# Token lists from SBUF marks, the weights' sort between tiles, and first-batch gathers and additions in the experts' last blocks

## What is computed

```python
x = x + _L0_xattn_ref(_layernorm(x), ctx_2048, ...)
x = x + _L0_ffn_ref(_layernorm(x), gate_weight, w_gate, w_up, w_down)
x = x + _L1_xattn_ref(_layernorm(x), ctx_2048, mask)
x = x + _L1_ffn_ref(_layernorm(x), gate_w, up_w, down_w, gate_s, up_s, down_s)

# the experts (E = 64, K = 8 of them per token, I = 192)
scores = softmax(x @ gate_weight.T)
topk_w, topk_idx = top_k(scores, K)
topk_w = topk_w / sum(topk_w)
# tokens sorted by expert, each expert: silu(g) * u through w_down
y = sum(outs * topk_w[:, :, None], axis=1)
```

## Time and profile before

| | us |
|---|---|
| median of three runs | 1570.71 |
| lowest, highest | 1570.06, 1575.04 |
| profiled execution, whole | 1574.58 |
| profiled execution, its span | 1572.8 |

### The profile page before, as it was taken

One profiled execution on the slowest core, in us unless ns is written; L12 is line 12 of the kernel. 1 busy time (PEld: TensorE's weight loads), 2 busy tenths in 40 slices (PEclk: granted clock), 3 DMA queues, 4 the chain that ended last, 5 costly groups with the idle time before them and its releaser, 6 DMA issues. The chain is left out here.

```text
span 1572.8 us, 37508 instructions
## 1 busy us (share of the span) xinstructions
PE 1414.7 (90%) x8673; PEld 1196.2 (76%) x8674; DVE 1027.5 (65%) x2067; ACT 905.3 (58%) x2048; POOL 615.0 (39%) x704
## 2 busy tenths in 40 slices
PE   7999899999843999999999999999981689999998
PEld 5887566667622888989898889888871578888888
DVE  5555488876687576777777666666635556766642
ACT  5555588873375576767676666766641334444442
POOL 1222387761142222222223233323217476666422
PEclk9999699999955999999999999999995799999999
DMA  6221791001171487878777877777638464444200
GB/s 220 81 88 54 262 362 53 2 5 54 54 314 31 158 275 275 286 265 293 259 256 271 288 251 251 263 237 261 228 113 281 140 180 136 134 137 135 80 14 28
DMA packets 93284, 278.19 MB, mean 177 GB/s; under 512 B 12757, under 2 KB 12886, under 8 KB 92502
## 3 DMA queue, kind: packets, MB, share of 16 engines
q1 hardware_dynamic: 69526, 199.67, 36.2%
q0 software_dynamic: 23680, 77.61, 16.0%
HBM read 209.07 MB, written 76.81 MB: 182 GB/s over the span
## 5 line engine op out<-in xcount | busy, mean ns | idle before, releaser
L1205 POOL DMA_INDIRECT xg<-h_rows,idx x168 | 180.8, 1076 | 463.9 <-PE m_x L1243 454.3
L1258 PE MATMUL m_g<-wgu_high,bxTh 128*128 x660 | 235.4, 357 | 3.5 <-DVE bxTl L1329 3.1
L1258 PE MATMUL m_g<-wgu_low,bxTh 128*128 x660 | 223.1, 338 | 0.0
L1258 PE MATMUL m_g<-wgu_high,bxTl 128*128 x660 | 223.0, 338 | 0.0
L1658 PE MATMUL f_g<-x4T_high,ffn_gu 128*128 128x256 f32 x704 | 176.6, 293 | 10.4 <-DVE f_hid L1836 5.9
L1658 PE MATMUL f_g<-x4T_low,ffn_gu 128*128 128x256 f32 x704 | 169.6, 282 | 0.0
L1329 DVE TENSOR_TENSOR bxTl<-m_x,bxTh 128x512 fp32r<-128x512 f32 x166 | 114.8, 692 | 81.0 <-ACT bxTh L1396 65.4
L1063 DVE TENSOR_TENSOR wgu_low<-raw_gu,wgu_high x61 | 107.3, 1759 | 82.6 <-ACT wgu_high L1053 79.3
L1414 ACT ACTIVATE y<-m_y 128x512 f32<-128x512 f32 x164 | 98.3, 600 | 104.4 <-PE m_y L1278 88.1
L1548 POOL DMA_INDIRECT G<-y_rows,slot x128 | 131.9, 1031 | 51.8 <-issue 47.5
L1278 PE MATMUL m_y<-wd_high,hidTm 128*128 x328 | 143.8, 439 | 5.2 <-DVE hidTm L1343 3.6
(11 more groups left out here) (264 smaller groups left out, 3312.7 us busy)
## 6 DMA issues: line engine op xcount, KB each, us to landing
raw_gu<-in_exp_gu SPq DMA_DIRECT2D x64, 768.0 KB, 6.6
y_rows<-y SPq DMA_DIRECT2D x164, 256.0 KB
raw_d<-in_exp_d SPq DMA_DIRECT2D x64, 512.0 KB, 7.4
y_rows<-zero SPq DMA_DIRECT2D x64, 256.0 KB, 3.4
ffn_gu<-ffn_gu_words SPq DMA_DIRECT2D x1, 5632.0 KB, 22.2
raw_c<-in_ctxT SPq DMA_DIRECT2D x16, 256.0 KB, 2.6
X<-in_x SPq DMA_DIRECT2D x4, 1024.0 KB, 5.7
h_rows<-h SPq DMA_DIRECT2D x16, 256.0 KB, 2.0
```

The costliest lines, as they stand in the source:

```text
L1205: eng.indirect_dma_start(xg[:, u, :].bitcast(F32), None, h_dram, bass.IndirectOffsetOnAxis(ap=idx[half][:, u:u + 1], axis=0)).then_inc(s_g ...
L1258: m = eng.matmul(pg[u % 2][:, 0:2 * I], xT[l][:, u % 2, c, :], W.gu[r][:, buf * DC + c, :], start=c == 0 and n == 0, stop=c == DC - 1 and ...
```

## The change

In *place*, the row numbers stay in SBUF as 16-bit (`it_row`), and `prow` with its copy is gone. For each tile ScalarE makes seven (tiles 0 to 11) or six (tiles 12 to 15) of the eight block signs, and VectorE the others, as (block number greater) times 2. The sort of the weights is cut into pieces that stand behind the marks of tiles 0 to 11. `marked` is made without waiting for the tables. The low splits of experts 0 to 2 and the high splits of experts 1 and 2 are taken out, and so are the loads of experts 3 and 4; they stand at the start of *experts*, the low ones on VectorE instead of GpSimd.

In *experts*, GpSimd issues behind its last token gather fourteen gathers of y (choices 0 to 6 of the two tiles of batch 0) into the buffers of the raw expert weights, three in flight; VectorE, behind its last block, adds them to X, and takes in the gathered bits of the down weights.

In *finish*, batch 0 gathers and adds only choice 7. SP waits for these two gathers before it loads memory, and the mask comes behind the memory. `find_exact` is in two parts that stand behind `negatives` and `maxima` of batch 0.

```diff
-            eng.wait_ge(s_tab, 1)
             eng.tensor_tensor(marked[:, :, :], mask16[:, :, :], order[:, :].unsqueeze(1).to_broadcast([P, NT, E]), ALU.mult).then_inc(s_mark, 1)
-            for n in range(NWB):
-                W.low_gu(eng, n, n)
-                W.low_d(eng, n, n)
...
-            eng.activation(prow[:, :], it_row[:, :], ACT.Copy).then_inc(s_row, 1)
...
-            for n in range(NWB - 1):
-                W.high_gu(eng, n, n)
-                W.high_d(eng, n, n)
+            W.high_gu(eng, 0, 0)
+            W.high_d(eng, 0, 0)
             eng.wait_ge(s_step, 1)
             for t in range(NT):
                 peL.wait(eng, t - 2, "list")
-                for k in range(K):
+                for k in range(K - STEPS(t)):
                     m = eng.activation(hotb[:, t % 2, k, :], it_blk[:, :], ACT.Sign, bias=step[:, t, k:k + 1])
                 actH.done(m, "hot")
-                if t == NT // 2:
-                    W.high_gu(eng, NWB - 1, NWB - 1)
-                    W.high_d(eng, NWB - 1, NWB - 1)
...
-            for n in range(NWB, NWB + 2):
-                W.raw_free(eng, n - NWB, s_apart)
-                W.load(eng, n, n - NWB, W.s_landing[NWB])
-                if n == NWB:
-                    W.landed(eng, W.s_landing[NWB], 1)
...
                 for k in range(K):
-                    m = eng.tensor_scalar(hotr[:, t % 2, k, :], prow[:, :], row_f[:, t, k:k + 1], tok_half[:, t:t + 1], ALU.is_equal, ALU.mult)
+                    eng.tensor_scalar(hotr[:, t % 2, k, :], it_row[:, :], row_f[:, t, k:k + 1], tok_half[:, t:t + 1], ALU.is_equal, ALU.mult)
+                for k in range(K - STEPS(t), K):
+                    m = eng.tensor_scalar(hotb[:, t % 2, k, :], it_blk[:, :], blk_f[:, t, k:k + 1], 2.0, ALU.is_gt, ALU.mult)
                 dveH.done(m, "hot")
+                if t in (0, 5):
+                    halves(t // 5)
+                if t in (1, 6):
+                    with_experts()
+                if t in (2, 7):
+                    sort(t // 5, range(NT // 2))
+                if t in (3, 8):
+                    sort(t // 5, range(NT // 2, NT))
+                if t in (4, 9):
+                    whole(t // 5)
+                if t == 4:
+                    sums()
+                if t == 10:
+                    placed()
+                if t == 11:
+                    weighted()
...
+            W.raw_free(eng, 0, s_apart)
+            W.load(eng, NWB, 0, W.s_landing[NWB])
+            W.landed(eng, W.s_landing[NWB], 1)
+            W.raw_free(eng, 1, s_apart)
+            W.load(eng, NWB + 1, 1, W.s_landing[NWB])
...
+            ends = [eng.value_load(endb[0:1, E - K + k:E - K + k + 1], min_val=E - K + k + 1, max_val=NBLK) for k in early]
...
+            eng.wait_ge(W.s_low_gu, E)
+            eng.wait_ge(W.s_low_d, E)
+            for k in early:
+                eng.wait_ge(s_y[0], (ends[k] + 1) // 2 * 16 + 16)
+                eng.wait_ge(s_y[1], ends[k] // 2 * 16 + 16)
+                apart(eng, s_apart)
+                for i in firsts:
+                    n = k * TPB + i
+                    if n >= AHEAD:
+                        eng.wait_ge(s_early[n % AHEAD], n // AHEAD * 16)
+                        apart(eng, s_apart)
+                    eng.indirect_dma_start(raw_rows[n], None, y_dram, bass.IndirectOffsetOnAxis(ap=slot8[:, i, k:k + 1], axis=0)).then_inc(s_early[n % AHEAD], 16)
...
+            W.low_gu(eng, 0, 0)
+            W.low_d(eng, 0, 0)
...
             turned(0, 0)
             turned(1, 1)
+            W.low_gu(eng, 1, 1)
             hidden(0, 0)
+            W.low_d(eng, 1, 1)
...
+                if first and u == 0:
+                    W.low_gu(eng, 2, 2)
...
+            for k in early:
+                for i in firsts:
+                    n = k * TPB + i
+                    eng.wait_ge(s_early[n % AHEAD], (n // AHEAD + 1) * 16)
+                    if k > 0:
+                        dveE.wait(eng, 0, f"k{k - 1}_{i}")
+                    dveE.done(eng.scalar_tensor_tensor(X[:, i, :], raw_rows[n], w8[:, i, k:k + 1], X[:, i, :], ALU.mult, ALU.add), f"k{k}_{i}")
...
+                if first and u == 0:
+                    W.high_gu(eng, 2, 2)
+                    W.high_d(eng, 2, 2)
...
+            W.high_gu(eng, 1, 1)
+            W.high_d(eng, 1, 1)
             silu(0, 0)
...
-            eng.dma_start(open8[:, :, :], a["mask"].unsqueeze(0).to_broadcast([P, B, S])).then_inc(s_m, 16)
+
+            for i in TI:
+                eng.wait_ge(s_g[i][K - 1], 16)
...
             load(0)
+            eng.dma_start(open8[:, :, :], a["mask"].unsqueeze(0).to_broadcast([P, B, S])).then_inc(s_m, 16)
...
-            gather(0, places)
+            gather(0, places[-TPB:])
...
-            find_exact()
-            add(0, adds)
+            add(0, adds[-TPB:])
             moments_a(0)
             scales_a(0)
+            eng.wait_ge(s_m, 16)
+            link(eng.tensor_reduce(valid[:, :], open8[:, :, :], axis=AX.X, op=ALU.max))
             negatives(0)
-            add(1, adds[:6])
+            find_odd()
+            add(1, adds[:2])
             maxima(0)
-            add(1, adds[6:9])
+            find_exact()
+            add(1, adds[2:9])
```

More of the change, by code:

```diff
@@ L989, in _, with halves, with_experts, sort @@
             eng.sem_inc(s_tab, 1)
-            eng.wait_ge(s_row, 1)
+            words = L[:, :, :].bitcast(I32)
+            def halves(n):
+                if n == 0:
+                    eng.wait_ge(s_exp, 1)
+                    link(eng.tensor_scalar(part[:, :, :], words, 16, None, ALU.arith_shift_right))
+                else:
+                    link(eng.tensor_scalar(part[:, :, :], words, 0xFFFF, None, ALU.bitwise_and))
+            def with_experts():
+                eng.wait_ge(s_mark, 1)
+                link(eng.tensor_tensor(both[:, :, :], part[:, :, :], marked[:, :, :], ALU.add))
+            def sort(n, tiles):
+                for t in tiles:
+                    last = eng.max(found[n][:, t, :], both[:, t, :])
+                link(last)
+            def whole(n):
+                link(eng.tensor_copy(bits[n][:, :, :], found[n][:, :, :]))
+            def sums():
+                link(eng.reduce_sum(total[:, :], e8[:, :, :], axis=AX.X))
+                link(eng.reciprocal(winv[:, :], total[:, :]))
+            def placed():
+                link(eng.tensor_scalar(bits[0][:, :, :], bits[0][:, :, :], 16, None, ALU.logical_shift_left))
+                link(eng.tensor_scalar(bits[1][:, :, :], bits[1][:, :, :], 0xFFFF, None, ALU.bitwise_and))
+            def weighted():
+                link(eng.tensor_tensor(bits[0][:, :, :], bits[0][:, :, :], bits[1][:, :, :], ALU.bitwise_or))
+                link(eng.tensor_tensor(w8[:, :, :], bits[0][:, :, :].bitcast(F32), winv[:, :].unsqueeze(2).to_broadcast([P, NT, K]), ALU.mult))
             for t in range(NT):
@@ L995, in _ @@
                 dveH.done(m, "hot")
[L999 to L1013, removed]
@@ L1363, in one, with blocks, bits_of, group @@
                 lows(b, u)
+                if first and u == 0:
+                    W.low_d(eng, 2, 2)
                 return e
[L1366 removed]
+            def blocks(i, first):
                 before = begun(eng, i * GB - 2)
                 for u in range(GB):
[L1369 removed]
+                    before = one(i * GB + u, u, before, first)
+            def bits_of(i, chunk):
+                dveB.wait(eng, i - 1, "bits")
+                dveB.done(eng.tensor_tensor(low_bits[:, :], low_bits[:, :], all_bits[:, bass.ts(chunk, D)], ALU.bitwise_or), "bits")
+            def group(i):
+                blocks(i, False)
                 with eng.If(i < 2 * FC):
[L1371 to L1372 removed]
+                    bits_of(i, eng.snap(i % (2 * FC), min_val=0, max_val=2 * FC - 1))
             used = used_groups(eng, endb)
[L1375 removed]
+            blocks(0, True)
+            bits_of(0, 0)
+            begin = WORDS_AT[0]
             for r, chunks in enumerate(rounds):
[L1377 to L1378 removed]
+                if begin < WORDS_AT[r]:
+                    with eng.Fori(begin, WORDS_AT[r]) as i:
+                        group(i)
                 eng.wait_ge(s_words[r], 16 * len(chunks))
@@ L1633, in read @@
                     peC.done(m, f"r{i}")
+            turn(0, "x3T", "n")
+            scores(0)
             eng.wait_ge(s_odd, 1)
-            eng.matmul(psc[0:1, 0, 0:1], odd[:, :], ones[:, :], start=True, stop=True).then_inc(s_sum, 1)
-            turn(0, "x3T", "n")
+            eng.matmul(py[0][0:1, 0:1], odd[:, :], ones[:, :], start=True, stop=True).then_inc(s_sum, 1)
+            turn_probs(0)
+            read(0)
             eng.wait_ge(s_exact, 1)
@@ L1640, in _ @@
             all_exact = eng.value_load(exact[0:1, 0:1], min_val=0, max_val=1)
-            scores(0)
-            turn_probs(0)
-            read(0)
             turn(0, "x4T", "n4_")
```

49 lines of the change are left out of this document (23 added, 26 removed).

## The result

The changed kernel takes 1560.2 us in the median (1558.47 to 1561.42) against 1570.43 before: the ratio is 0.9925, 95% interval 0.991 to 0.9941. It is faster, by 10.2 us, where 29.0 were forecast; 1541.7 and the range up to 1552 are both missed. The profiled execution took 1561.42 us with a span of 1559.7 us, against 1574.58 and 1572.8: in spans 13.1 us less. The profiled execution of before lay 4 us above its median, the new one 1.2, hence the difference to 10.2.

What follows compares the result with a forecast made beforehand. TensorE, busy 90% of the span, was taken as the bound, so only its idle holes could be won: -17.5 + 1.5 + 6.8 - 19.8 = -29.0, taking the median from 1570.71 to 1541.7 us; 8-in-10 range 1535 to 1552.

Steps and rivals of the forecast that it cites:

- part 1: Placing stage: marks from 16-bit SBUF row numbers come every 0.15 us, 1.2 us a tile instead of 2.64.
- first rival: Placing: marks from SBUF stay dear; at 0.22 us place wins 10, total 1549; chance 0.2 with its dearer cases.
- part 3: Placing: VectorE's 10.6 us sort goes in pieces between tiles; lists at 485.3 against 504.24, 17.5 us left after unevenness.
- part 4: Splits and loads moved into the experts' start: those under the first gather cost nothing; 1.5 us (0 to 4) in all.
- The experts' start: Expert 2's splits make silu 1 2 us late and block 3's low parts some 3; cost 1.5 us (0 to 4).
- part 5: Experts' end: fourteen early gathers, 1.43 us each from 1164, end the block 6.8 us later (5 to 11).
- the tail gives its gain back: Rival: experts' end stretches by 12 to 15 us, or memory and mask hold the scores; 1547 to 1552; chance 0.12.
- part 6: Last stage with two gathers: mask lands at about 14 us, batch 0's maxima start at 20 instead of 39.8, 19.8 earlier.
- The slower rival: Experts' end: in-flight limit serialises early gathers, block ends 45 us late, total 1580; chance 0.04 with other such stalls.

Runs made afterwards that it cites:

- e6: Changed kernel with a mark's second scalar made the constant 0.5, so lists are wrong; one execution, no ratio; place 50.18 us.
- e7: Changed kernel with the marks' row numbers back in PSUM as fp32, sort between tiles kept; ratio 0.9981 to the kernel before.
- e4: Changed kernel with the low split of expert 0 back on GpSimd in the placing stage; ratio 0.9941 to the kernel before.
- e8: Changed kernel with VectorE's low split of expert 0 held by a wait on GpSimd's first gathers, expert 3's load behind it; ratio 0.9864 to the kernel before.
- e5: Changed kernel with the mask's load issued at the last stage's start, ahead of SP's wait for the two gathers; ratio 0.9892 to the kernel before.
- e3: Changed kernel with seven early gathers in flight instead of three; ratio 0.9958 to the kernel before.

## Why the prediction was wrong

It was right on the sign and on what each edit does, but all five terms of its sum came out worse than it had them. Four misses count: the largest is the experts' end, then the price of a mark, the zero for what lies under the first gather, and the last stage.

- **The price of a mark** (part 1): the failed step of place. Between 0.10 and 0.33 us it took 0.15, from the nearest row by size, an operation of 128 columns from SBUF. That row's scalars are constants, while a mark reads two from SBUF. It measured 0.224. The forecast's first rival had this case, "at 0.22 place wins 10", and it won 12.0; 5.5 of the missing 15.9 us are here. e6 and e7 show it, with one thing changed each: marks of 0.163 and 0.32 us. In e6 place gains 18.0 us, so with a mark near 0.15 the rest of part 3 would have held.
- **Splits and load under the first gather** (part 4, "nothing"): +3.5. The row that covered them shows how long a gather takes beside an idle VectorE; the split was costed against time and not against the engine that it ran beside (+2.4). The load of expert 3 was seen but taken as no worse than the ffn_d words that it replaces; the landing is 2.0 longer, of which e4 against before gives 1.2 for the load in place of the words. The steps between the lists and the gather are 0.8 shorter. e8 removes both, e4 the first.
- **The experts' start**: 1.5 forecast, 1.6 measured. The second silu is 2.1 us late, as forecast (10.88 behind the first transposition, before 8.77), and the first y 0.8. The match of the sum is luck in part: this stretch differs by up to 5.7 us between profiles on other chips (666.4 to 672.1).
- **The experts' end** (part 5): 6.8 forecast, 14.5 measured, the largest miss. The forecast's own times give 7.2 (1186.4 and 0.8, less 1179.98), not 6.8. GpSimd came free at 1164.6 in the old time (1155.95, moved by the 8.7 us gained ahead of it), as forecast at 1164. The pace failed: 22.87 us from first to fourteenth instead of 18.4, +4.5. Their waits are for landings: four carry the name of y's stores, and by the code the third gather before is what they wait for; the landings took up to 5.6 us in this stretch, where 4.0 had been taken from the rows of the token gathers. And the way out of the stage was left out: the sum ended the stage with the last addition, 4.8 us behind the start of the fourteenth gather, and the last stage starts 7.6 behind it, a constant distance of 6.66 from that gather's end. Before, GpSimd's last gather of the experts was long done and the last store ended the stage. The other profiles put the same two steps at 20.7 to 21.7 us of pace and 7.6 to 7.9 of way out. The rival "the tail gives its gain back" with 12 to 15 us named this, and came to pass at 0.12.
- **The last stage** (part 6): 19.8 forecast, 17.8 measured. The mask had been put 14 us into the stage, 12.9 behind the first gather, and landed at 15.3; `valid` could not start before. e5 shows what hung on it, 2.2 to 2.9 us in its own group.
- **The slower rival** did not come: the three in flight do overlap. Its opposite did: without the limit the experts slow down (e3).

The terms: place 5.5, first gather 3.5, experts' end 7.7, last stage 2.0, start of the experts 0.1, less 2.9 for the stretches in which nothing was forecast, make 15.9, the difference between 29.0 and 13.1 in spans. The 2.9 lie in stretches without an edit and are luck in the kernel's favour. The range was too narrow for a plain reason: the errors were taken as alternatives, one rival at a time, while three of them came together.

## What to carry to other kernels

An operation is costed by the nearest row in all of its operands, the scalars that it reads from memory included, and not by its columns. A split that "fits under" a wait is free only if the engine beside it doesn't use the same memory path; look which of VectorE and GpSimd both work from SBUF there. When work is moved over the edge between two stages, look which engine leaves the stage last (here GpSimd, 6.7 us behind its last gather) and count as saved only what ran under the last block: of fourteen gathers, seven were issued there.

## What the runs showed of the hardware

- A scalar read from SBUF costs VectorE about 61 ns per operation (0.224, 0.163 us for two and one).
- A VectorE operation of 0.23 us (one fp32 source in SBUF) takes 3.24 and 2.26 us beside a two-input operation of GpSimd's; MAX8 doesn't stretch (2.13 us for sixteen), nor do marks from PSUM. A gather of GpSimd's takes 3.59 or 2.51 us instead of 1.23 or 0.95 beside VectorE's two-input splits, and 1.23 beside its clearings.
- The last stage starts 6.65 to 6.66 us behind the end of GpSimd's last early gather in seven of eight profiles with three in flight, and 3.06 to 3.33 behind VectorE's last addition; 0.73 where the additions end late (e3).
- A comparison of 1024 16-bit columns with two SBUF sources takes 0.69 us, a multiplication by a scalar 0.49; together they come every 1.13 us in place of eight marks in 1.79.
- In the one profile with seven gathers in flight instead of three, the distance of two y goes from 3.9 to 10.7 us.
